# Second attention: VectorE sorts another head's candidates ahead of the wait for the near values

## The reference

```python
# second attention of the reference (L1_attn); x is (4, 1024, 128)
hd = Dx // Hh                      # 128 // 16 = 8
topk = max(1, int(Tx * 0.3))       # 307 of 1024
scale = Dx ** (-0.5)
qkv = x @ W_qkv.T + b_qkv
...
scores = jnp.einsum('bhid,bhjd->bhij', q, k) * scale
topk_scores, indices = jax.lax.top_k(scores, topk)
...
masked = jnp.full_like(scores, -jnp.inf)
masked = masked.at[bi, hi, ti, indices].set(topk_scores)
attn = jax.nn.softmax(masked, axis=-1)
out = jnp.einsum('bhij,bhjd->bhid', attn, v)
out = jnp.transpose(out, (0, 2, 1, 3)).reshape(Bx, Tx, Dx)
return out @ W_out.T + b_out
...
x = L0_attn_x
x = x + _L0_attn_ref(_layernorm(x, axis=-1), ...)
x = x + _L0_ffn_ref(_layernorm(x, axis=-1), ...)
x = x + _L1_attn_ref(_layernorm(x, axis=-1), ...)
x = x + _L1_ffn_ref(_layernorm(x, axis=-1), ...)
```

## Time and profile before

| | us |
|---|---|
| median of 3 runs | 3609.91 |
| lowest and highest | 3607.0 and 3611.21 |
| profiled execution | 3602.09 |
| its span | 3600.4 |

### The profile page before, as it was taken

The page is one execution under the profiler, slowest core; times in us unless marked ns, Lnnn a source line. Parts: engine busy times, 40 slices in busy tenths (PEclk is TensorE's granted clock), DMA queues, the critical chain, the costliest instruction groups (busy, mean ns, idle before and its releaser), DMA issues. The chain is left out here.

```text
span 3600.4 us, 75874 instructions
## 1 busy us (share of the span) xinstructions
PE 2754.6 (77%) x23657; PEld 1541.3 (43%) x23705; DVE 2734.2 (76%) x9130; ACT 2480.5 (69%) x4051; POOL 1960.2 (54%) x4543
## 2 busy tenths in 40 slices
PE   4699999677736777777777777776777787757999
PEld 2233333233513454544444545444445454544444
DVE  5777777226448999999999999998999999844444
ACT  2266666433138999999999999997999999832222
POOL 3133333410237777787877777776777777730000
PEclk8699999888656767677777676776776667677999
DMA  5221111010130101101100100110100110010000
GB/s 156 74 53 48 48 53 28 11 33 26 62 54 2 15 3 17 17 2 17 17 7 12 17 14 5 17 15 3 17 11 7 17 15 3 2 31 0 9 6 9
DMA packets 115274, 85.95 MB, mean 24 GB/s; under 512 B 58153, under 2 KB 97339, under 8 KB 114875
## 3 DMA queue, kind: packets, MB, share of 16 engines
q1 hardware_dynamic: 106331, 75.20, 9.7%
q0 software_dynamic: 8192, 4.79, 0.9%
q10 hardware_dynamic: 352, 1.18, 0.1%
HBM read 54.25 MB, written 19.40 MB: 20 GB/s over the span
## 5 line engine op out<-in xcount | busy, mean ns | idle before, releaser
L1285 POOL TENSOR_TENSOR a_near<-a_side,a_z 128x1024 int32<-128x1024 int32 x512 | 968.3, 1891 | 42.7
L1181 PE MATMUL a_ST<-a_qs,a_ks 75*128 75x128 bf16 x4096 | 749.8, 271 | 305.2 <-ACT a_eT L1220 215.3
L1381 DVE MAX8 a_cand<-a_near 128x8 f32<-128x256 f32 x2048 | 778.1, 406 | 2.6 <-POOL a_near L1285 2.5
L1181 PEld LDWEIGHTS a_ST<-a_qs,a_ks 75*128 75x128 bf16 x4096 | 504.8, 125 | 513.7 <-issue 507.0
L1420 DVE TENSOR_SCALAR_CACHE_REDUCE a_z<-a_S,a_thr 128x1024 f32<-128x1024 f32 x512 | 645.6, 1261 | 77.7 <-issue 56.2
L1205 ACT ACTIVATE a_signs<-a_z,a_tiny 128x1024 bf16<-128x1024 f32 x512 | 587.4, 1147 | 152.0 <-DVE a_z L1420 151.2
L1198 ACT ACTIVATE a_signs<-a_S,search 128x1024 bf16<-128x1024 f32 x512 | 569.2, 1112 | 23.1 <-PE a_S L1134 23.0
L1220 ACT ACTIVATE a_eT<-a_ST 128x1024 f32<-128x1024 f32 x512 | 518.7, 1013 | 59.7 <-PE a_ST L1182 59.1
L1134 PE MATMUL a_S<-a_ks,a_qs 72*128 72x512 bf16 x1024 | 438.1, 521 | 99.4 <-DVE a_z L1420 75.6
L775 ACT ACTIVATE a_eT<-a_ST 128x512 f32<-128x512 f32 (+3 forms) x768 | 354.0, 489 | 212.1 <-PE a_ST L745 159.0
L879 DVE TENSOR_REDUCE a_mx<-a_S 128x1 f32<-128x512 f32 (+3 forms) x768 | 380.9, 548 | 92.9 <-PE a_S L732 56.2
(11 more groups left out here) (342 smaller groups left out, 4568.5 us busy)
## 6 DMA issues: line engine op xcount, KB each, us to landing
a_qs<-q_parts SPq DMA_DIRECT2D x174, 64.0 KB
a_ks<-k_parts SPq DMA_DIRECT2D x174, 64.0 KB
a_qs<-a_flip SPq DMA_DIRECT2D x512, 0.8 KB
q_parts<-p_qp SPq DMA_DIRECT2D x48, 128.0 KB, 1.7
k_parts<-p_kp SPq DMA_DIRECT2D x48, 128.0 KB, 1.8
a_qs<-q_parts SPq DMA_DIRECT2D x60, 96.0 KB
a_ks<-k_parts SPq DMA_DIRECT2D x60, 96.0 KB
f_w<-L_ffn_W SPq DMA_DIRECT2D x16, 256.0 KB, 2.9
```

The source lines that it names most:

```text
L1181: pe.matmul(ST[:, block_of], ks[:, base(hl) + kb * P:base(hl) + (kb + 1) * P], qs[:, tile(hl):tile(hl) + P], start=True, stop=False)
L1285: pool.tensor_tensor(near[:, hl % 2, :].bitcast(I32), side[:, one].bitcast(I32).broadcast_to([P, SEQ]), z[:, hl % H, :].bitcast(I32), ALU. ...
L1381: mm = dve.max(found[:, 8 * g:8 * g + 8], near[:, h2 % 2, g * SW:(g + 1) * SW])
```

## The change

In every slot sort_first moves to directly behind z, with the wait for the candidate list in front of it. first_sorted and sort_rest follow, ahead of the wait for the near values. What stood ahead of the sort moves behind that wait: the ranks' comparison (h mod 4 = 0). The mask (odd h) keeps its place behind the wait, but now has the first two sorting steps ahead of it, and in slots with h mod 4 = 1 the transpose too. The reciprocal (h mod 4 = 2) now follows sort_first, and the context follows sort_rest. sort_last and the four maxima follow behind; the maxima stand in a row in odd slots. All idle copies go, except the one ahead of the load of the flags' sum. The wait of `top_in` has its condition written differently, which changes nothing here, as the loop's numbers are all known when it is unrolled. No other engine's code is touched.

```diff
--- before.py
+++ after.py
@@ -1410,35 +1410,32 @@
                     if has3 is not None:
                         dve.max(ranked[:, 8:16], rest[:, :]).then_inc(sort_s, 1)
 
-                def past_waits(c):
-                    dve.tensor_copy(idle[:, 2 * (h % H) + c:2 * (h % H) + c + 1], half[0:1, :])
-
                 if has1 is not None:
                     dve.wait_ge(thr1_s, l1 + 1)
                     if h1 % 2 and not (isinstance(it, int) and l1 < H):
                         dve.wait_ge(mask_a, it * (UN // 2) + (h - C2) // 2 - (H // 2 - 1))
                     dve.tensor_scalar(z[:, h1 % H, :], S[h1 % 2][:, :], thr1[:, h1 % H:h1 % H + 1], None, ALU.add, ALU.max,
                                       accum_out=zmax[:, h1 % H:h1 % H + 1]).then_inc(z_s, 1)
+                listed()
+                sort_first()
                 if h % 4 == 0:
-                    listed()
+                    first_sorted()
+                    sort_rest()
+                    near_made()
                     if has4 is not None:
                         dve.wait_ge(rank_s, l4 + 1)
                         dve.wait_ge(sort_s, SORTS * l4 + SORTS)
                         dve.tensor_tensor(hits[:, :, :], odd2[:, :].rearrange("p (o r) -> p o r", o=1).broadcast_to([P, 4, WINDOW]),
                                           wide(rank[:, four], WINDOW), ALU.is_equal).then_inc(choice_s, 1)
-                    sort_first()
-                    first_sorted()
+                    rest_made()
+                    sort_last()
                     if has4 is not None:
                         dve.wait_ge(choice_s, 2 * q4 + 1)
                         dve.tensor_tensor(picked[:, :, :], hits[:, :, :], best[:, ring4, :], ALU.mult).then_inc(choice_s, 1)
-                    sort_rest()
-                    rest_made()
-                    near_made()
+                    top(0)
                     if has4 is not None:
                         dve.wait_ge(choice_s, 2 * q4 + 2)
                         dve.tensor_reduce(edge[:, four], picked[:, :, :], AX, ALU.add).then_inc(edge_s, 1)
-                    sort_last()
-                    top(0)
                     top(1)
                     if has4 is not None:
                         open_ends = cand[:, ring4, :].rearrange("p j (g r) -> p j g r", r=8)[:, :, :, 7]
@@ -1449,7 +1446,14 @@
                     top(2)
                     top(3)
                 elif h % 2:
-                    listed()
+                    if lagged(it, h, TOPL, UN, TOTAL) is not None and ends(h, TOPL):
+                        q, ring = quad(it, h, TOPL), ((h - TOPL) // 4) % 2
+                        dve.wait_ge(part_s, PART_STEPS * q + PART_STEPS)
+                        if not (isinstance(q, int) and q < 2):
+                            dve.wait_ge(top_in, 16 * 4 * (q - 1))
+                        dve.transpose(flip[:, ring, :], parts[:, ring, :]).then_inc(flip_s, 1)
+                    first_sorted()
+                    sort_rest()
                     near_made()
                     if lagged(it, h, PICK, UN, TOTAL) is not None:
                         dve.wait_ge(cut_s, it * QU + (h - PICK) // 4 + 1)
@@ -1457,42 +1461,25 @@
                             dve.wait_ge(turned, lp - (MASKS - 1))
                         dve.tensor_scalar(mask[:, hp % MASKS, :], z[:, hp % H, :], cut[:, hp % H:hp % H + 1], AWAY,
                                           ALU.is_lt, ALU.mult).then_inc(mask_s, 1)
-                    sort_first()
-                    top(0)
-                    first_sorted()
-                    if lagged(it, h, TOPL, UN, TOTAL) is not None and ends(h, TOPL):
-                        q, ring = quad(it, h, TOPL), ((h - TOPL) // 4) % 2
-                        dve.wait_ge(part_s, PART_STEPS * q + PART_STEPS)
-                        if not (isinstance(it, int) and q < 2):
-                            dve.wait_ge(top_in, 16 * 4 * (q - 1))
-                        dve.transpose(flip[:, ring, :], parts[:, ring, :]).then_inc(flip_s, 1)
-                    else:
-                        past_waits(0)
-                    sort_rest()
-                    top(1)
                     rest_made()
-                    past_waits(1)
                     sort_last()
-                    top(2)
-                    top(3)
+                    for g in range(SEGS):
+                        top(g)
                 else:
                     q, hn = quad(it, h, NL), here(h, NL + 3) % H
                     norm = lagged(it, h, NL, UN, TOTAL) is not None
-                    listed()
                     if norm:
                         dve.wait_ge(ot, q + 2)
                         dve.reciprocal(rden[:, hn:hn + 4], heads[:, :, HD]).then_inc(rd, 1)
-                    sort_first()
                     first_sorted()
+                    sort_rest()
                     near_made()
                     if norm:
                         dve.wait_ge(rd, q + 1)
                         dst = ctx_all.rearrange("p t (g c) -> p (t g) c", c=32)[:, bass.ds(q, 1), :].rearrange("p o (j d) -> p (o j) d", d=HD)
                         dve.tensor_tensor(dst, heads[:, :, 0:HD], wide(rden[:, hn:hn + 4], HD), ALU.mult).then_inc(normed, 1)
-                    sort_rest()
                     top(0)
                     rest_made()
-                    past_waits(0)
                     sort_last()
                     top(1)
                     top(2)
@@ -1504,7 +1491,7 @@
                     if closes(it, h):
 
                         dve.wait_ge(flag_v, group + 1)
-                        past_waits(1)
+                        dve.tensor_copy(idle[:, 2 * (h % H) + 1:2 * (h % H) + 2], half[0:1, :])
                         total = dve.value_load(flag_sum[0:1, 0:1].bitcast(I32), min_val=0, max_val=2 ** 31 - 1)
                         with dve.If(total > 0):
                             dve.tensor_reduce(flags[:, :], FL.rearrange("p (j c) -> p j c", c=VIEWS), AX, ALU.add)
```

## The result

| | before | after |
|---|---|---|
| median us | 3608.45 | 3559.78 |
| lowest, highest | 3606.57, 3611.21 | 3557.75, 3563.89 |
| profiled execution's span | 3600.4 | 3557.4 |

The ratio is 0.9866, with a 95% interval of 0.9849 to 0.9883. The medians differ by 48.7 us, the two profiled spans by 43.0. The interval of the ratio is a gain of 42 to 54 us. The forecast was 3562, from a gain of 48; for the profiled execution it was 3554, and that took 3559.1.

The account below looks back on a forecast made before the run. VectorE and ScalarE, both nearly full, lose time waiting for each other. 37 x 0.68 + 27 x 0.90 = 49.5 us, rounded to 48, so 3610 - 48 = 3562 us; range 3520 to 3594.

Parts of the forecast that it names:

- The chain near values, mask, VectorE's work, z, ScalarE in slots 1 and 5 sets the time: Second attention: twice in a group of eight slots, this chain holds ScalarE up; shortening it saves 0.39 us each time.
- the piece through TensorE in slot 6: Slot 6, long groups: z, reciprocal, sort, context, TensorE's flag product, masked scores, then ScalarE's exponential, 0.85 us late.
- 0.39 us off each: Slots 1 and 5: mask's start to next z falls from 2.48 to 2.07 us, a saving of 0.41, taken as 0.39.
- Sorting is hidden, match and transpose run free beside the near values: Slots 1 and 5: moved work of about 0.38 us fits in idle time before the mask, not slowed by GpSimd.
- Slots 0, 3 and 4 count for nothing: Slots 0 and 4 save 0.30 us off the chain; slot 3's z is also in time; all counted as zero.
- rival 1: The chain in slots 0, 3, 4 counts as well: VectorE saves 1.97 us a group, 3485 to 3540 us; chance 0.13.
- the term of 0.35 us: One part, its slot not named, of the 1.97 us a group that VectorE saves in rival 1's sum.
- The context 0.10 us later, the near wait in front of it covered by 0.38 us of sorting: Slots 2 and 6: context at z + 0.38 instead of z + 0.29 us; delays TensorE by 0.10 in slot 6.
- Copies: 0.05 us each, those off the chain free: Each copy delays its follower by 0.05 us: 26 us of VectorE time, mostly off the chain, the rest already counted.
- 37 long groups, 27 short ones: Of 64 groups of eight slots, long ones (33.0 us) save 0.68 us each, short ones (32.16 us) 0.90 each.
- One of the signs that I gave against the forecast: Forecast is wrong if ScalarE's waits for TensorE grow by what its waits for z lose.
- one that I gave for it: In the profile after, TensorE's wait for the context should shrink by 0.68 us a group.

Follow-up runs that it names:

- e1: The kernel before, with the changed order only in slots with h mod 4 = 1 and no copy there: 3571.2 us, ratio 0.9893.
- e2: The changed kernel, with slots with h mod 4 = 1 put back to the old order and their copy: 3612.7 us, ratio 1.0011.
- e7: The changed kernel, with TensorE's masked scores moved ahead of its flag product: 3520.5 us, ratio 0.9758 to the kernel before.
- e9: e1 without the idle copies: 3565.1 us, ratio 0.9883 to the kernel before.
- e5: The changed kernel, with the near wait of slots with h mod 4 = 2 moved behind the context: 3539.3 us, ratio 0.9810 to the kernel before.
- e11: The changed kernel, with GpSimd's cut moved behind the near values and rank of its slot: 3535.5 us, ratio 0.9797 to the kernel before.
- e8: e6 and e7 together: 3514.9 us, ratio 0.9752 to the kernel before.
- e6: The changed kernel, with reciprocal, sort_first, context, then match and near wait in slots with h mod 4 = 2: 3537.6 us, ratio 0.9804 to the kernel before.

## Why the prediction was right, point by point

- *The chain near values, mask, VectorE's work, z, ScalarE in slots 1 and 5 sets the time.* Right, and shown from both sides: e1 keeps 38 us of 49 with these slots alone, e2 keeps none without them. It is not the only chain: e7 leaves these slots alone and takes 39 us more off, from the piece through TensorE in slot 6.
- *0.39 us off each.* Right: 2.48 became 2.08, and ScalarE's waits for z fell by 0.41 and 0.45 us. The sum of these waits, forecast at about 100 us, is 95.9.
- *Sorting is hidden, match and transpose run free beside the near values.* Right. Minimum, median and maximum in ns of the match, the transpose and the comparison, in the changed kernel:

```profile
L1403 DVE MATCH_REPLACE8 a_rest<-a_best,a_cand x512: 174/176/179, 1057.3 to 3106.2; 128x32 f32<-128x32 f32 x171
...
L1454 DVE STREAM_TRANSPOSE a_flip<-a_parts x128: 184/194/201, 1063.5 to 3102.4; 128x32 bf16<-128x32 bf16 x128
...
L1428 DVE TENSOR_TENSOR a_hits<-a_odd,a_rank x128: 213/224/227, 1074.3 to 3107.1; 128x64 f32<-128x64 f32 x128
```

  The transpose at 2096.26 lies wholly inside the near values and took 0.20. This agrees with the Trainium skill (SBUF — State Buffer, Who interferes with whom), by which a VectorE instruction with one SBUF input, outside the two-port modes, doesn't contend with GpSimd. The comparison, with two inputs, is at 224 ns in the median where it was 516.
- *Slots 0, 3 and 4 count for nothing.* Not contradicted: e2 gives nothing; e9 leaves up to 5 us open. In rival 1's sum the term of 0.35 us, by its place that of slot 3, has no working in the prediction.
- *The context 0.10 us later, the near wait in front of it covered by 0.38 us of sorting.* **This step failed.** The context started 0.36 us later instead of 0.10 (0.34 in the mean of the undisturbed groups). I had shifted z by 0.39 against the near values; the shift measured 0.66 us (in the mean over the undisturbed groups the near values ended 0.11 us ahead of the end of z in slot 6, now 0.55 behind), and it has two parts. VectorE gets from the end of near values to the end of the next z in 0.46 us less: 0.40 in the work, and 0.06 because the mask starts 0.04 us behind the near values and not 0.10. And GpSimd's next near values start 0.21 us later behind the last, which I had not looked for. In the kernel before, from the near values that end at 2020.75 (start, length, line):

```profile
2020.85 0.19 POOL L1259 TENSOR_TENSOR a_scaled<-a_sgn,search 128x1 f32<-128x1 f32 x1
2021.12 0.53 POOL L1261 TENSOR_TENSOR a_thr<-a_scaled,search 128x1 f32<-128x1 f32 x1
...
2022.58 1.89 POOL L1285 TENSOR_TENSOR a_near<-a_side,a_z 128x1024 int32<-128x1024 int32 x1
```

  In the changed kernel, from those that end at 2097.31:

```profile
2097.41 0.73 POOL L1259 TENSOR_TENSOR a_scaled<-a_sgn,search 128x1 f32<-128x1 f32 x1
2098.23 0.19 POOL L1261 TENSOR_TENSOR a_thr<-a_scaled,search 128x1 f32<-128x1 f32 x1
...
2099.35 1.89 POOL L1285 TENSOR_TENSOR a_near<-a_side,a_z 128x1024 int32<-128x1024 int32 x1
```

  The mask holds a GpSimd step that comes while it runs. Before, GpSimd's first step (L1259) and the mask both started at 2020.85, the step took its usual 0.19, and only the second (L1261) was stretched, to 0.53. With the mask 0.06 us ahead (2097.35), the first is stretched to 0.73 and the second follows it. The undisturbed groups agree: in slot 5 the two starts lay within 0.01 us of each other before, and L1259 took at most 0.19; now the mask is 0.06 ahead and L1259 takes at least 0.73. From the end of one near value to the start of the next it was 1.83 us and is 2.04. The same appears in e1, where only slots 1 and 5 have the new order (mean end 0.56 behind z), so it belongs to them. e5 and e11 show that the late near values were what cost the context its time. The long group gained 0.54 us and not 0.68, the short one 0.78 and not 0.90. No run keeps the GpSimd step from being stretched while the mask is early, so the 0.21 us is read from the traces and not tested alone.
- *Copies: 0.05 us each, those off the chain free.* The size was near or somewhat low: 9 us (5 to 12) and 12 us where I had 6. That copies off the chain are free is argued; no run takes out those alone. Over the whole kernel 542 copies went, not 512, as the loop has a tail. By the Trainium skill (VectorE: DVE Perf Modes, The DRAIN you can't avoid) a semaphore between two VectorE instructions costs nothing extra. In the changed kernel the reciprocal, which doesn't wait for the sort, starts 0.10 behind it (2083.61 to 2083.71), while in the earlier trace rows the context behind a wait took 0.20, so for such short instructions the rows still disagree. The prediction left out what the same section adds, that a next instruction that is not held starts before the pipe is empty; the 0.05 behind a copy and the 0.10 behind a sort go with that, and so don't speak against the section.
- *37 long groups, 27 short ones.* Too coarse. The undisturbed groups lie anywhere between 31.9 and 33.4 us before the change and between 31.0 and 32.5 after it. Before, 27 of the 59 are 32.9 us or longer, after it 17 are 32.4 or longer. So although both ends lost less than forecast, the mean fell from 32.60 to 31.87, by 0.73 us, close to the 0.77 that the forecast comes to (49.5 / 64). The two errors, a smaller saving in each kind of group and fewer long groups, nearly cancelled: that 3562 came so close to 3559.8 was luck, and 2 us is also less than the interval of the measurement can tell.
- *One of the signs that I gave against the forecast came true in part*: ScalarE's waits for TensorE grew by 24 us, not by all of the 55 that its waits for z lost. And one that I gave for it failed: TensorE's wait for the context should have shrunk by 0.68 us a group, some 43 us. In the kernel before and in the changed one it was:

```profile
PE a_OT L1162 <- DVE ctx L1491: 169.7, 61, 3.7
```

```profile
PE a_OT L1162 <- DVE ctx L1480: 172.4, 61, 3.3
```

  It did not shrink. In e5, with the context early again, it is 148.1 us.

## What to carry to other kernels

When a wait is late by a fixed amount in some slots of a pipeline, independent short work in front of it is free there, and in the other slots it only shifts who waits. Before counting a gain, follow the freed instruction to every other wait that it now reaches earlier than its data: here a wait that had cost nothing, in front of a result that another engine needed, took 20 us until it was moved one line down, or its data came earlier. Then look at the queue of the engine that waits for that result, and let what doesn't depend on it go first: that gave 39 us by itself (e7), and 23 us on top of the early context (e8 against e6).

## What the runs showed of the hardware

- A VectorE instruction with two SBUF inputs was held to the end of GpSimd's 1.89 us operation (up to 1114 ns for work of 201 ns), while MAX8, the match, the transpose and the reciprocal ran beside it at their usual times.
- A copy of one value, recorded at 0.12 us, delays its follower by 0.05 us. 542 of them cost 9 us (5 to 12) in a stage where VectorE was busy for 90% of the time.
- The holding goes both ways. A GpSimd step of 0.19 us took 0.73 us when VectorE's mask (128x1024, f32 to bf16, 0.75 us) had started 0.06 us ahead of it, and kept its 0.19 when the two started within 0.01 us of each other. A mask that starts earlier can so delay the very values that the next slot waits for.
